# A two-layer decoder: the mix product with its weight stationary and in a new order, the sign weight made during the experts, the decay clamp on GpSimd

## The chip, the cores and the metric

The kernel runs on one core of a Trainium2 chip. The metric is the device time of one execution in microseconds (us). The engines that matter here are TensorE (PE; PEld is its weight load), VectorE (DVE), ScalarE (ACT) and GpSimd (POOL); SP only issues transfers.

## The reference, cut to what matters

The input x has 8 batches of 100 tokens and 256 features, the context 361 tokens for each batch. Six blocks follow one another, each on a layernorm of the stream x, each added to it: a self attention with contextual positions, a cross attention, a mixture of 8 experts, a gated recurrence, a cross attention with 16 heads, and a product with a ternary weight. The change touches blocks 4 and 6:

```python
aiv = x @ W_aiv                       # 256 -> 3 * 1024
a_proj, i_proj, v = jnp.split(aiv, 3, axis=-1)
a = jax.nn.sigmoid(a_proj + decay_bias)
i = jax.nn.sigmoid(i_proj)
input_signal = jnp.sqrt(jnp.maximum(1.0 - a * a, 1e-08)) * (i * v)
h = _chunked_scan(a, input_signal)    # along the 100 tokens, in chunks of 64
return h @ W_mix + b_mix              # 1024 -> 256
...
w_ternary = jnp.clip(jnp.round(w / scale), -1.0, 1.0)   # scale = max(mean |w|, 1e-5)
return jnp.einsum('bsi,oi->bso', x, w_ternary * scale)
```

## The kernel before

All engines have one instruction stream each, written by hand, and meet by semaphores. The program goes through the blocks in order.

**Experts and gather.** The experts' results go to memory (`slots_out`) and GpSimd fetches them back, one indirect DMA for each batch (L748). VectorE adds each to X (L1818), takes statistics and, for the first four batches, normalises as soon as GpSimd has made `rstd` by a power (`rsqrt(3, 0)`, L655, between the seventh and the eighth fetch). TensorE transposes the result into XT. Before that `side("gather")` makes the last value projections of block 5 and one column sum `f`, and `keep_warm` issues products that nobody reads.

**Recurrence.** The 1024 channels are 8 tiles j of 128 partitions; along the free axis lie 8 batches of 101 columns (one reset column each). TensorE makes for each j three gate products `aiv(n, g)` (L1388): the decay w=0, the input gate w=1, the value w=2, in two halves g of 400 tokens; the order is the list `AIV`. They use four pairs of PSUM banks, and item n waits until item n-4 was read. ScalarE turns w=0 and w=1 into DEC and UU by sigmoid (L967, L969), squares the clamped decay (L976) and takes the root (L980). VectorE does for each j: `decay(j)` = clamp of DEC to 1e-10..1 (L1838), one column for each batch into BT (L1845), a scan (L1848); `inputs(j-1)` = L1828 and the scan of the state L1831, after which `state` counts j; `gated(j)` = product with the value in PSUM (L1860, it gives `iv_done`) and L1862. After `gated(1)` it also makes the ternary weight WN (L1879 to L1884). GpSimd adds the mix bias to two batches of X (L768) after each of the first four states. It also clears the two BT buffers before the stage (L761 to L763).

**Mix product.** `mix(p, j)` (L1421) adds tile j to the result of the two batches of p, once `state` has reached j+1. UU is the stationary operand (100 tokens of one batch) and the 256 columns of W_mix move, so that the result lies with tokens on partitions and `x_add(p)` (L1892) adds it to X. TensorE does p=0 for all j, p=1 for all j, p=2 for all j, four half steps of p=3 (`mix_last`), and then starts block 5; twelve half steps of p=3 are filled into block 5's plan at ticks 0 to 22. After `x_add(p)` follow statistics, `rstd` on GpSimd (L774), normalisation (L1908), `x_tr(p)` (L1441), ScalarE's copy (L1008), the query product `q_mm(p)` (L1451), and `q_out(p)`, which gives the first of three bf16 parts of the queries. VectorE (p=0) or GpSimd (p=1 to 3) makes the other two parts; all are stored to memory and loaded back in another layout (L574, L440) before the first score product `maxima(0, 0)` (L1495) may start.

**Block 5** runs by the tables `PLAN` and `ONCE` in ticks, sixteen for a batch. For the first batch its first step is the row maximum on VectorE (L1934).

## Time and profile before

| | us |
|---|---|
| runs, median | 443.76 |
| runs, lowest and highest | 437.52, 448.41 |
| the profiled execution, its device time | 437.58 |
| its span, first to last instruction | 435.8 |
| gate products, start to end | 219.0 to 286.6 |
| mix products, start until block 5 starts | 286.6 to 316.6 |

The profile page gives a share of the span to each engine: PE 93%, DVE 61%, ACT 40%, POOL 31%. A window row gives the busy time of each engine in a stretch and the granted clock of TensorE, 1.00 for 2.4 GHz and 0.50 for 1.2 GHz. A timeline row gives start, length, engine, line, operation, operands and their shapes; `[2.00 <-DVE RC L1831]` behind it says that the engine was idle 2.00 us until that instruction ended. Three runs lie 11 us apart.

### The profile page before, as it was taken

To read this page: it belongs to the slowest core of one execution; us is meant where nothing else is said; L and a number is where in the kernel's file an instruction comes from. 1 tells how busy PE (TensorE), PEld (TensorE's weight loads), DVE (VectorE), ACT (ScalarE), POOL (GpSimd) and SP (SyncE) were. 2 spreads that over 40 slices of the span, in tenths; PEclk is the share of its full clock that TensorE was granted. 3 is DMA by queue.
4 is the path that set the end of the run, shared out by engine and by line. 5 is a ranking of instruction groups with operands and counts; after the bars stand their busy time and mean duration, and the time that the engine had idled before them with its cause. 6 is when DMAs were issued, how large, how long until landed. Compare 5 with 4: busy or idle time off the path is not lost.

```text
span 435.8 us, 7507 instructions
## 1 busy us (share of the span) xinstructions
PE 405.3 (93%) x2967; PEld 265.5 (61%) x2967; DVE 267.7 (61%) x475; ACT 174.9 (40%) x362; POOL 137.1 (31%) x188
## 2 busy tenths in 40 slices
PE   6999998995999998899699999989998999999896
PEld 2556664563556866697455555557765766666564
DVE  4159658899324552012855999992498677777334
ACT  0440351110431237342338367521105666666651
POOL 3852007763530044812700112000035473300200
PEclk9899999999999998999979999998999999999999
DMA  7994001111860065345200000055645437320001
GB/s 219 393 271 149 4 0 51 55 50 51 252 184 2 2 268 196 101 126 157 57 2 0 0 1 2 0 108 112 186 124 137 123 89 169 95 53 4 3 20 58
DMA packets 32850, 42.19 MB, mean 97 GB/s; under 512 B 7712, under 2 KB 29132, under 8 KB 32418
## 3 DMA queue, kind: packets, MB, share of 16 engines
q1 hardware_dynamic: 29897, 34.18, 26.5%
q0 software_dynamic: 2304, 5.76, 5.2%
q10 hardware_dynamic: 614, 1.77, 2.0%
q8 instruction: 24, 0.39, 0.4%
q14 instruction: 11, 0.09, 0.1%
HBM read 33.00 MB, written 8.98 MB: 96 GB/s over the span
## 4 chain that ended last, share of the span: by engine, by line
PE 56%; DVE 22%; issue 7%; DMA 5%; ACT 5%; POOL 3%; SPq 1%; POOLq 0%; DVEq 0%; ACTq 0%
PE banks L1421 5%; PE banks L1541 4%; PE banks L1105 4%; PE banks L1167 4%; PE banks L1526 4%; PE banks L1495 3%; PE banks L1255 3%; DVE NM L1934 3%; PE banks L1192 3%; PE banks L1388 2%; PE banks L1290 2%; PE banks L1308 2%; DVE RA L493 2%; DVE RC L1862 2%; DVE RC L1828 2%
## 5 line engine op out<-in xcount | busy, mean ns | idle before, releaser
L1934 DVE TENSOR_REDUCE NM<-banks 100x2 f32<-100x722 f32 x64 | 56.4, 903 | 19.5 <-PE banks L1495 19.2
L1388 PE MATMUL banks<-XT,RBG 128*128 128x400 f32 x192 | 67.3, 513 | 0.2 <-ACT XT L833 0.2
L1388 PEld LDWEIGHTS banks<-XT,RBG 128*128 128x128 f32 x192 | 37.4, 196 | 29.6 <-issue 3.1
L1046 ACT ACTIVATE CT<-banks 128x400 f32<-128x400 f32 (+1 forms) x72 | 35.8, 504 | 24.4 <-PE banks L1526 23.0
L1421 PE MATMUL banks<-W,RC 128*100 128x256 f32 x128 | 32.3, 395 | 2.0 <-DVE RC L1831 2.0
L1693 DVE TENSOR_TENSOR RC<-RV 128x800 f32<-128x800 f32 x16 | 19.3, 1278 | 14.2 <-ACT RV L875 14.2
L1421 PEld LDWEIGHTS banks<-W,RC 128*100 128x100 f32 x128 | 22.0, 175 | 8.3 <-DVE RC L1831 2.4
L1255 PE MATMUL banks<-RC,SELT 128*128 128x400 f32 x64 | 24.0, 508 | 2.7 <-DVE RC L1747 2.0
L1541 PE MATMUL banks<-CT,RV 128*17 128x100 f32 (+1 forms) x576 | 24.0, 254 | 0.0
L1616 DVE BATCH_NORM_STATS2 st<-X 100x6 f32<-100x256 f32 x48 | 19.5, 423 | 6.9 <-DMA X<-in_x 5.8
L655 POOL TENSOR_TENSOR rstd<-ve,mhalf 100x4 f32<-100x4 f32 x8 | 8.5, 1057 | 47.8 <-DVE ve L1625 47.8
L1145 PE MATMUL banks<-W,CT 128*128 128x256 f32 (+1 forms) x96 | 21.3, 381 | 0.7 <-DVE RC L1814 0.5
L1814 DVE TENSOR_TENSOR RC<-banks,RC 100x256 f32<-100x256 f32 x8 | 3.4, 424 | 28.6 <-PE banks L1377 28.6
L1145 PEld LDWEIGHTS banks<-W,CT 128*128 128x128 f32 (+1 forms) x96 | 17.5, 184 | 4.7 <-DVE RC L1814 0.9
L1255 PEld LDWEIGHTS banks<-RC,SELT 128*128 128x128 f32 x64 | 11.6, 189 | 12.8 <-DVE RC L1747 5.2
L768 POOL TENSOR_TENSOR X<-X,RB 100x512 f32<-100x512 f32 x4 | 5.1, 1272 | 45.5 <-DVE RC L1831 45.5
L1152 PE MATMUL banks<-onesb 128*128 128x512 bf16 x57 | 16.7, 435 | 2.4 <-POOL onesf L643 2.4
L1134 PE MATMUL banks<-CT,W 128*128 128x361 f32 x48 | 17.7, 521 | 1.1 <-issue 1.1
L1747 DVE TENSOR_TENSOR RC<-banks,RV 128x800 f32<-128x800 f32 x16 | 15.6, 984 | 4.2 <-PE banks L1255 4.2
L1526 PE MATMUL banks<-RC,RA 100*128 100x100 bf16 (+1 forms) x192 | 16.6, 210 | 1.3 <-DMA RC<-NT 1.3
L833 ACT ACTIVATE XT<-banks 128x800 f32<-128x800 f32 x8 | 6.6, 841 | 27.9 <-PE banks L1094 27.9
L774 POOL TENSOR_TENSOR rstd<-ve,mhalf 100x2 f32<-100x2 f32 x4 | 2.8, 702 | 46.9 <-DVE ve L1902 46.9
(259 smaller groups left out, 852.0 us busy)
## 6 DMA issues: line engine op xcount, KB each, us to landing
RA<-in_L_ffn_W SPq DMA_DIRECT2D x2, 2048.0 KB, 11.6
RBG<-in_L_attn_W_aiv SPq DMA_DIRECT2D x1, 3072.0 KB, 12.4
CT<-in_ctx_t SPq DMA_DIRECT2D x2, 1444.0 KB, 11.3
k_parts<-RA SPq DMA_DIRECT2D x12, 180.5 KB, 3.4
RA<-k_parts SPq DMA_DIRECT2D x12, 180.5 KB, 3.5
RBG<-k_parts POOLq DMA_DIRECT2D x12, 180.5 KB, 4.2
RA<-k_parts POOLq DMA_DIRECT2D x12, 180.5 KB, 3.9
RBG<-in_ctx SPq DMA_DIRECT2D x2, 1024.0 KB, 17.6
```

What stands on the lines that cost most here:

```text
L1046: sc.activation(P4[slot][0:n, g * HG * T:(g + 1) * HG * T], PS[4 + w % 2][0:n, 0:HG * T], ACT.Exp).then_inc(st_exp, 1)
L1105: ins = mm(bank[0:T, 0:D], lhs(k), rhs(k), start=(k == 0), stop=(k == KT - 1))
L1134: ins = mm((lo, hi)[m][:, 0:S], W4[:, 0, k, m * P:(m + 1) * P], CT[:, k, b * S:(b + 1) * S], start=(k == 0), stop=(k == KT - 1))
L1145: ins = mm(o, CT[:, k, b * S + s0:b * S + s0 + n], W4[:, 1, k, :], start=(k == 0), stop=(k == KT - 1))
L1255: ins = mm(PS[2 * (u % 2) + g][:, 0:GC], SELT[:, u], AL[:, GB * g:GB * g + GB].rearrange("p s t -> p (s t)"), start=True, stop=True)
L1388: ins = mm(PS[2 * aiv_pair(j, w) + g][:, 0:GC], WA[:, k, c:c + P], XT[:, k, GC * g:GC * g + GC], start=(k == 0), stop=(k == KT - 1))
L1421: ins = mm(PS[MIX_BANK[p]][0:T, b % 2 * D:b % 2 * D + D], UU[:, j, b, 1:TP], WMIX[:, j, :], start=(j == 0 and b % 2 == 0), stop=(j == RT - ...
L1526: ins = mm(PS[4 + w % 2][0:n, c * T:c * T + T], KS[b % KSLOTS][0:KROWS, h, s0:s0 + n], queries(KROWS, h, b), start=True, stop=True)
L1541: ins = mm(PS[6][32 * c:32 * c + VW, g * T:g * T + T], V4[0:n, NJ * b + j, h, :], P4[(NJ * b + j) % PSLOTS][0:n, h * T:h * T + T], start=( ...
L1616: v.bn_stats(st6[:, b], X[:, b]).then_inc(stats_done, 1)
L1693: v.tensor_tensor(PB[u % 5], k0[:, k].rearrange("p (s t) -> p s t", s=B), q0[:, k, s * T:s * T + T].unsqueeze(1).broadcast_to([P, B, T]), ...
L1934: v.tensor_reduce(NM[:, b % 2, 2 * i:2 * i + 2], PP[w % 2][0:T, :, 0:S], AX.X, ALU.max, negate=True).then_inc(mx_out, 1)
```

## The change

Three edits, with what they carry along.

1. **Mix product.** W_mix becomes the stationary operand (two halves of 128 output features), the 200 tokens of two batches move. The result has features on partitions. ScalarE copies it to XT (`mix_evac`), TensorE transposes it back into the same bank (`mix_tr`, four transposes), and `x_add` follows as before. TensorE's order is new: p=0 up to j=6, p=1 up to j=5, then (0,7), (1,6), (1,7), then `mix_tr(0)`, p=2, and twelve half steps of p=3, with the transposes and query products set between them. Four half steps of p=3 stay in the plan (ticks 0 to 3), `mix_evac(3)` and `mix_tr(3)` come at ticks 23 and 26. On VectorE `x_add(1)`, `ln_stats(1)` and `ln_norm(1)` now come ahead of the split of query 0.
2. **Sign weight.** WN is made while VectorE waits for the first expert. For that the column sum `f` moves from the last to the second place in the list `SIDE`. `keep_warm` ahead of the transposes of block 4 issues 14 products, not 5.
3. **Clamp.** For j of 2 and more, clamp and BT column are made by GpSimd, which also waits for `iv_done` of j-1. The four bias adds now follow the clamps of j=2 to 5. The clearing of BT moves from GpSimd to ScalarE, ahead of its first copy of XT; `rsqrt(3, 0)` comes after the eighth fetch.

```diff
-            keep_warm(PS[2], 5)
+            keep_warm(PS[2], 14)
...
             def mix(p, j, both=(0, 1)):
                 pe.wait_ge(state, j + 1)
-                for b in (2 * p + c for c in both):
-                    ins = mm(PS[MIX_BANK[p]][0:T, b % 2 * D:b % 2 * D + D], UU[:, j, b, 1:TP], WMIX[:, j, :],
-                             start=(j == 0 and b % 2 == 0), stop=(j == RT - 1), skip_group_check=True)
-                    if j == RT - 1:
-                        ins.then_inc(y_mm, 1)
+                for m in both:
+                    ins = mm(PS[MIX_BANK[p]][:, QC * m:QC * m + QC], WMIX[:, j, m * P:(m + 1) * P],
+                             UU[:, j, 2 * p:2 * p + 2, 1:TP], start=(j == 0 and m == 0), stop=(j == RT - 1),
+                             skip_group_check=True)
+                if j == RT - 1 and both[-1] == 1:
+                    ins.then_inc(mix_mm, 1)
                 return ins
+
+            def mix_tr(p):
+                pe.wait_ge(mix_out, p + 1)
+                for b in (2 * p, 2 * p + 1):
+                    for m in range(KT):
+                        c0 = b % 2 * D + m * P
+                        ins = nc.tensor.transpose(PS[MIX_BANK[p]][0:T, c0:c0 + P], XT[:, m, b * T:b * T + T], identf[:])
+                    ins.then_inc(y_mm, 1)
...
-            for j in range(RT):
+            for j in range(RT - 1):
                 mix(0, j)
-            for j in range(RT):
+            for j in range(RT - 2):
                 mix(1, j)
-                if j == 3:
-                    x_tr(0)
-                if j == 4:
-                    q_mm(0)
+            mix(0, RT - 1)
+            for j in (RT - 2, RT - 1):
+                mix(1, j)
+            mix_tr(0)
             pe.wait_ge(iv_done, RT - 1)
             for j in range(RT):
                 mix(2, j)
-                if j == 3:
-                    x_tr(1)
-                if j == 4:
-                    q_mm(1)
+                if j == 1:
+                    mix_tr(1)
+                elif j == 4:
+                    x_tr(0)
+                elif j == 5:
+                    q_mm(0)
...
-            for i in range(4):
+            for i in range(12):
                 ins = mix_last(i)
-            ins.then_inc(uu_used, 1)
+                if i == 3:
+                    ins.then_inc(mix_mm, 1)
+                    mix_tr(2)
+                elif i == 5:
+                    x_tr(1)
+                elif i == 7:
+                    q_mm(1)
...
+            def mix_evac(p):
+                act.wait_ge(mix_mm, p + 1 + p // 3)
+                src = PS[MIX_BANK[p]][:, 0:KT * QC].rearrange("p (k n) -> p k n", k=KT)
+                sc.activation(XT[:, :, QC * p:QC * p + QC], src, ACT.Copy).then_inc(mix_out, 1)
...
-                if b == B - 2:
-                    rsqrt(3, 0)
+            rsqrt(3, 0)
...
-            for p in range(B // 2):
+            def mix_bias(p):
                 pool.wait_ge(xn_ready, 4 * B)
-                pool.wait_ge(state, p + 1)
                 gp.tensor_tensor(X[:, 2 * p:2 * p + 2], X[:, 2 * p:2 * p + 2],
...
+            for j in range(2, RT):
+                pool.wait_ge(clamped, j)
+                pool.wait_ge(sig, SIG_AT[j, 0])
+                pool.wait_ge(iv_done, j - 1)
+                a_j, bt = DEC[:, j], BT[j % 2]
+                link(gp.tensor_scalar(a_j[:, :, 1:TP], a_j[:, :, 1:TP], FLOOR, 1.0, ALU.max, ALU.min))
+                gp.tensor_scalar(bt[:, :, 1 + CHUNK:2 + CHUNK], a_j[:, :, 1 + CHUNK:2 + CHUNK], 1.0 / FLOOR, None,
+                                 ALU.mult).then_inc(clamped, 1)
+                if j < 2 + B // 2:
+                    mix_bias(j - 2)
```

The order on VectorE in the recurrence, from `gated` of one tile to the scan of the decay two tiles on (RC holds UU, RA holds DEC, CT holds BT and the square roots; "x100" shapes are the clamp). Before:

```order
L1860 TENSOR_TENSOR RC<-RC,banks 128x8x100 [waits aiv_mm,sig]
L1862 SCALAR_TENSOR_TENSOR RC<-CT,RC 128x808 [waits iv_done]
L1838 TENSOR_SCALAR RA<-RA 128x8x100 [waits sig,dve_link]
L1845 TENSOR_SCALAR CT<-RA 128x8 [waits clamped]
L1848 SCALAR_TENSOR_TENSOR CT<-RA,CT 128x808 [waits dve_link]
L1828 SCALAR_TENSOR_TENSOR RC<-CT,RC 128x808 [waits roots,dve_link]
```

and after the change:

```order
L1907 TENSOR_TENSOR RC<-RC,banks 128x8x100 [waits aiv_mm,sig]
L1909 SCALAR_TENSOR_TENSOR RC<-CT,RC 128x808 [waits iv_done]
L1899 SCALAR_TENSOR_TENSOR CT<-RA,CT 128x808 [waits clamped,dve_link]
L1870 SCALAR_TENSOR_TENSOR RC<-CT,RC 128x808 [waits roots,dve_link]
L1873 SCALAR_TENSOR_TENSOR RC<-RA,RC 128x808 [waits u_done]
```

The clamp and the BT column are gone from VectorE, and its scan waits for `clamped`. On GpSimd, from the last fetch to the second tile, before:

```order
L748 DMA XN<-slots_out,small 100x256 x6
L655 TENSOR_TENSOR rstd<-ve,mhalf 100x4 [waits var_ready]
L748 DMA XN<-slots_out,small 100x256
L758 MEMSET RA 128x64 [waits k_st3,k_st2,side_mm]
L759 MEMSET RC 128x64
L761 MEMSET CT 128x808
L761 MEMSET CT 128x808 [waits pool_link]
L762 MEMSET CT 128x8 [waits pool_link]
L763 MEMSET CT 128x8
L655 TENSOR_TENSOR rstd<-ve,mhalf 100x4 [waits var_ready]
L768 TENSOR_TENSOR X<-X,RB 100x512 [waits state,xn_ready] x4
```

and after:

```order
L656 TENSOR_TENSOR rstd<-ve,mhalf 100x4 [waits var_ready]
L758 MEMSET RA 128x64 [waits k_st3,k_st2,side_mm]
L759 MEMSET RC 128x64
L656 TENSOR_TENSOR rstd<-ve,mhalf 100x4 [waits var_ready]
L772 TENSOR_SCALAR RA<-RA 128x8x100 [waits iv_done,sig,clamped]
L773 TENSOR_SCALAR CT<-RA 128x8 [waits pool_link]
L763 TENSOR_TENSOR X<-X,RB 100x512 [waits xn_ready]
L772 TENSOR_SCALAR RA<-RA 128x8x100 [waits iv_done,sig,clamped]
L773 TENSOR_SCALAR CT<-RA 128x8 [waits pool_link]
```

The power (`rstd`) moved behind the eighth fetch, the clearing of CT is gone, and a clamp (RA), a BT column (CT) and a bias add (X) now stand in turn, the clamp waiting for VectorE's `iv_done`.

On TensorE, what stands around the first transposes (banks2 is the bank pair of p=0 and p=1, banks3 that of p=2 and p=3, W0 holds W_mix, RC holds UU, W4 the query weights). Before, step (1,3), the transposes x_tr(0), step (1,4) and the query product q_mm(0):

```order
L1421 MATMUL banks2<-W0,RC 100x256 [waits state]
L1421 MATMUL banks2<-W0,RC 100x256
L1441 MATMUL banks0<-identf,XN 128x100 [waits xn_ready,sig]
L1441 MATMUL banks0<-identf,XN 128x100
L1441 MATMUL banks0<-identf,XN 128x100 [waits xn_ready]
L1441 MATMUL banks0<-identf,XN 128x100
L1421 MATMUL banks2<-W0,RC 100x256 [waits state]
L1421 MATMUL banks2<-W0,RC 100x256
L1451 MATMUL banks0<-XT,W4 128x200 [waits unit_xt]
L1451 MATMUL banks0<-XT,W4 128x200 x3
```

and after the change, step (1,7), mix_tr(0), the steps (2,0) and (2,1), and mix_tr(1):

```order
L1439 MATMUL banks2<-RC,W0 128x200 [waits state]
L1439 MATMUL banks2<-RC,W0 128x200
L1451 MATMUL banks2<-identf,XT 100x128 [waits mix_out]
L1451 MATMUL banks2<-identf,XT 100x128 x3
L1439 MATMUL banks3<-RC,W0 128x200 [waits state,iv_done]
L1439 MATMUL banks3<-RC,W0 128x200
L1439 MATMUL banks3<-RC,W0 128x200 [waits state]
L1439 MATMUL banks3<-RC,W0 128x200
L1451 MATMUL banks2<-identf,XT 100x128 [waits mix_out]
L1451 MATMUL banks2<-identf,XT 100x128 x3
```

`x_add(0)`, which came right behind step (0,7), now waits for mix_tr(0), with the steps (1,6) and (1,7) between them. The step (0,7), the first that needs the eighth state, stood eighth in the stream and now stands fourteenth; x_tr(0) moved from behind (1,3) to behind (2,4).

## Rows read from the trace of the kernel before

**Rows 1.** Busy time by stretch: window, length, five engines, granted clock, DMA share, GB/s

```profile
212.00:214.00 2.00, 0.00 (x0) 0.00 (x0) 1.78 (x7) 1.17 (x2) 1.04 (x1) 1.00 0.19 64
...
217.00:219.00 2.00, 1.45 (x5) 0.55 (x5) 1.93 (x7) 0.84 (x1) 0.28 (x3) 0.50 0.00 0
219.00:224.00 5.00, 5.00 (x8) 2.61 (x9) 2.93 (x11) 0.59 (x1) 1.04 (x1) 0.53 0.00 0
...
295.40:298.80 3.40, 3.40 (x10) 2.31 (x9) 1.80 (x7) 0.00 (x0) 0.53 (x1) 0.50 1.02 220
```

**Rows 2.** Timeline, last two state scans on VectorE, then TensorE

```profile
288.12 1.84 DVE L1831 TENSOR_TENSOR_SCAN RC<-RA,RC 128x808 f32<-128x808 f32 x1
...
292.94 1.84 DVE L1831 TENSOR_TENSOR_SCAN RC<-RA,RC 128x808 f32<-128x808 f32 x1
...
294.83 6.25 PE L1421 MATMUL banks<-W,RC 128*100 128x256 f32 x20 [2.00 <-DVE RC L1831]
```

**Rows 3.** Timeline of one tile of the scan: start, length, engine, line, shape [idle<-releaser]

```profile
253.91 0.96 DVE L1860 TENSOR_TENSOR RC<-RC,banks 128x800 f32<-128x800 f32 x1
254.14 1.27 POOL L768 TENSOR_TENSOR X<-X,RB 100x512 f32<-100x512 f32 x1 [8.68 <-DVE RC L1831]
...
254.91 1.36 DVE L1862 SCALAR_TENSOR_TENSOR RC<-CT,RC 128x808 f32<-128x808 f32 x1
...
256.30 0.58 DVE L1838 TENSOR_SCALAR RA<-RA 128x800 f32<-128x800 f32 x1
...
257.12 1.84 DVE L1848 TENSOR_TENSOR_SCAN CT<-RA,CT 128x808 f32<-128x808 f32 x1
...
260.03 1.84 DVE L1831 TENSOR_TENSOR_SCAN RC<-RA,RC 128x808 f32<-128x808 f32 x1
...
278.53 1.00 DVE L1862 SCALAR_TENSOR_TENSOR RC<-RA,RC 128x808 f32<-128x808 f32 x1
```

**Rows 4.** Timeline, VectorE, first and last of the six sign-weight instructions

```profile
246.34 0.15 DVE L1879 TENSOR_SCALAR fs<-fs 128x1 f32<-128x1 f32 x1
...
247.82 0.69 DVE L1884 TENSOR_TENSOR WN<-WN,WF 128x512 f32<-128x512 f32 x1
```

**Rows 5.** Timeline, TensorE, mix product, its transposes and the query product

```profile
286.62 6.21 PE L1421 MATMUL banks<-W,RC 128*100 128x256 f32 x28
...
300.91 0.51 PE L1441 MATMUL banks<-identf,XN 100*128 100x100 f32 x4
...
302.13 1.52 PE L1451 MATMUL banks<-XT,W 128*128 128x200 f32 x8
...
316.80 0.47 PE L1495 MATMUL banks<-RBG,RA 97*100 97x361 bf16 x2
```

**Rows 6.** Timeline around the last gather and the first gate products

```profile
213.89 3.38 DVE L1630 TENSOR_SCALAR XN<-X,mv,rstd 100x256 f32<-100x256 f32 x4
...
214.08 1.18 POOL L748 DMA_INDIRECT XN<-slots_out,small  x1 [0.23 <-issue]
...
219.00 5.28 PE L1388 MATMUL banks<-XT,RBG 128*128 128x400 f32 x8 [0.22 <-ACT XT L833]
...
220.62 1.38 DVE L1630 TENSOR_SCALAR XN<-X,mv,rstd 100x256 f32<-100x256 f32 x4 [1.17 <-POOL rstd L655]
```

**Rows 7.** Timeline of VectorE, then of GpSimd, where the two meet

```profile
65.52 1.85 DVE L1733 TENSOR_TENSOR RC<-RC,RA 128x800 f32<-128x800 f32 x1
...
66.58 1.43 POOL L694 CAST RA<-RA 128x722 bf16<-128x722 f32 x1
...
75.16 0.79 POOL L694 CAST RA<-RA 128x722 bf16<-128x722 f32 x1
```

**Rows 8.** Groups of instructions, GpSimd: count, busy us, mean ns

```profile
L709 POOL TENSOR_SCALAR mkx<-mki 8x361 bf16<-8x361 int32 x1 | 1.5, 1487 | 5.5 <-DMA mk<-in_mask_keep 5.5
```

**Rows 9.** Timeline of the SP queue, then the query loads of L440

```profile
307.93 1.88 SPq L440 DMA_DIRECT2D RA<-q_parts  x3
...
DMA to landing us min/median/max: 2.4/2.8/7.8
```

More of the change, by code:

```diff
@@ L330, in build @@
         q4_first = sem("q4_first")
-        uu_used = sem("uu_used")
+        mix_mm = sem("mix_mm")
+        mix_out = sem("mix_out")
         aiv_half = sem("aiv_half")
@@ L363, in __call__ @@
                 self.eng.wait_ge(self.sem, self.n)
-        SIDE = ([("qk", 0)] + [("k", b) for b in range(B)] + [("v", b) for b in range(B)] + [("f", 0)])
-        SIDE_AT = {"cope": 1, "soft": 3, "spread": 5, "ln1": 6, "ln2": 7, "router": 8, "route": 13, "gather": 18}
-        SIDE_LOW = [1, 3, 4, 8, 10, 12, 14, 16]
-        SPREAD_AT = {4: (3, 0), 5: (3, 1), 9: (4, 0), 10: (4, 1)}
+        SIDE = ([("qk", 0), ("f", 0)] + [("k", b) for b in range(B)] + [("v", b) for b in range(B)])
+        SIDE_AT = {"cope": 1, "soft": 4, "spread": 6, "ln1": 7, "ln2": 8, "router": 9, "route": 14, "gather": 18}
+        SIDE_LOW = [2, 4, 5, 9, 11, 13, 15, 17]
+        SPREAD_AT = {4: (4, 0), 5: (4, 1), 9: (5, 0), 10: (5, 1)}
         def side_bank(i):
@@ L405, in build @@
         PLAN_END = TICKS * (B - 1) + 60
-        ONCE = ([("mix_last", 2 * i if i < 14 else 2 * i - 11, 4 + i) for i in range(2 * RT - 4)]
-                + [("ln_norm", 15, 2), ("x_tr", 18, 2), ("x_out", 18, 2), ("q_mm", 20, 2), ("q_out", 20, 2),
+        ONCE = ([("mix_last", i, 12 + i) for i in range(4)]
+                + [("ln_norm", 15, 2), ("x_tr", 18, 2),
+                   ("x_out", 18, 2), ("q_mm", 20, 2), ("q_out", 20, 2), ("mix_evac", 23, 3), ("mix_tr", 26, 3),
                    ("x_add", 27, 3), ("zero_bank", 28, 0), ("ln_stats", 31, 3), ("ln_norm", 36, 3),
@@ L416, in build @@
         ORDER = ("q_mm", "x_tr", "x_out", "q_out", "x_add", "zero_bank", "ln_stats", "ln_norm", "parts", "sums_tr",
-                 "normalise", "out_tr", "out_mm", "maxima", "scores", "weighted", "os_evac", "add", "mix_last",
+                 "normalise", "out_tr", "out_mm", "maxima", "mix_evac", "mix_tr", "scores", "weighted", "os_evac", "add", "mix_last",
                  "last")
@@ L758, in _ @@
             gp.memset(DEC[:, :, :, 0:1], 0.0)
[L759 to L763 removed]
+            gp.memset(UU[:, :, :, 0:1], 0.0).then_inc(consts, 1)
             rsqrt(3, 1)
[L765 removed]
+            def mix_bias(p):
                 pool.wait_ge(xn_ready, 4 * B)
[L767 removed]
                 gp.tensor_tensor(X[:, 2 * p:2 * p + 2], X[:, 2 * p:2 * p + 2],
@@ L953, in _ @@
             sc.activation(BQ16[:, 0:1], BQ16[:, 0:1], ACT.Sigmoid)
+            for t in BT:
+                link(sc.activation(t, onesf[:, 0:1].unsqueeze(2).broadcast_to([P, B, TP]), ACT.Copy, scale=0.0))
+                sc.activation(t[:, :, 0:1], onesf[:, 0:1].unsqueeze(2).broadcast_to([P, B, 1]), ACT.Copy,
+                              scale=1.0 / FLOOR)
             xt_out(xn_tr, 3 * G, xt_ready, [0])
-            act.wait_ge(consts, 6)
+            act.wait_ge(consts, 7)
             def gate(j, w, groups=range(G)):
@@ L1027, in q_out @@
                 ins.then_inc(q4_out, 1)
+            def mix_evac(p):
+                act.wait_ge(mix_mm, p + 1 + p // 3)
+                src = PS[MIX_BANK[p]][:, 0:KT * QC].rearrange("p (k n) -> p k n", k=KT)
+                sc.activation(XT[:, :, QC * p:QC * p + QC], src, ACT.Copy).then_inc(mix_out, 1)
+            mix_evac(0)
+            mix_evac(1)
             x_out(0)
             q_out(0)
+            mix_evac(2)
             act.wait_ge(qs_one[0], 16)
@@ L1034, in _ @@
             q_out(1)
[L1035 removed]
+            act.wait_ge(mix_mm, NQ)
             load_queries(act, 1, 0)
@@ L1075, in last_xt @@
                 sc.activation(XT[:, :, b0 * T:b1 * T], src, ACT.Copy).then_inc(unit_xt, 1)
-            run_block4(scores=exps, parts=parts_out, os_evac=os_evac, out_tr=ot_evac, x_out=x_out, q_out=q_out,
+            run_block4(scores=exps, parts=parts_out, os_evac=os_evac, out_tr=ot_evac, x_out=x_out, q_out=q_out, mix_evac=mix_evac,
                        last_xt=last_xt)
@@ L1600, in _ @@
             run_block4(maxima=maxima, parts=parts_tr, scores=scores, weighted=weighted,
-                       sums_tr=sums_tr, out_tr=out_tr, out_mm=out_mm, mix_last=mix_last, x_tr=x_tr, q_mm=q_mm,
+                       sums_tr=sums_tr, out_tr=out_tr, out_mm=out_mm, mix_last=mix_last, mix_tr=mix_tr, x_tr=x_tr, q_mm=q_mm,
                        last_tr=last_tr, last_mm=last_mm, fill=lambda: keep_warm(PS[4], 2))
@@ L1851, in decay @@
             def decay(j):
-                dve.wait_ge(sig, SIG_AT[j, 0])
-                reset_scan(j, 1 if j < 2 else None)
+                if j < 2:
+                    dve.wait_ge(sig, SIG_AT[j, 0])
+                    reset_scan(j, 1)
+                else:
+                    dve.wait_ge(clamped, j + 1)
+                    link(v.tensor_tensor_scan(flat(CD[j % 2]), flat(DEC[:, j]), flat(BT[j % 2]), 0.0, ALU.mult,
+                                              ALU.max))
             def gated(j):
@@ L1913, in _ @@
             ln_norm(0)
+            x_add(1)
+            ln_stats(1)
+            ln_norm(1)
             dve.wait_ge(q4_out, 1)
@@ L1918, in _ @@
             v.tensor_tensor(QP[0][:, 2], QW[0], QP[0][:, 1], ALU.subtract).then_inc(q4_split, 1)
-            x_add(1)
-            ln_stats(1)
-            ln_norm(1)
             x_add(2)
```

32 lines of the change are left out of this document (12 added, 20 removed).

## The prediction

> **What bounds the kernel now.** I began with the chain of waits from the end. Between 286 and 317 us it leaves TensorE once: it goes back from the mix product to VectorE's last state scan. The timeline shows what that costs: TensorE has stood for 2.0 us when it starts at 294.83 [rows 2], and by the table of windows it then runs at clock 0.50 from 295.4 to 298.8 [rows 1]. VectorE is late because its tiles lie back to back: product 0.96, L1862 1.36, clamp and BT column 0.85, scan 1.84, 1.07 until the state scan, and that 1.84, together 7.9 us [rows 3]. The gate products don't wait for it, only the tail does. The second place is the start of the gate products: TensorE has nothing from 212 to 214, is at 0.50 by 217, and its first eight gate instructions take 5.28 us, 0.66 each, where the mean clock of the stretch is 0.53 [rows 1, 6]. The third is the mix stretch itself, where TensorE is the bound: it runs without a gap from 294.83 until the first score product at 316.80 [rows 2, 5].
>
> The sum is made against the profiled execution's 437.58 us. That is the fast end of the three runs; their median lies 6.2 us above it, so I carry the difference over as a ratio.
>
> **Gather and first gate products.** The eighth fetch (1.18 us) now comes ahead of the power, not behind it; the power waited for VectorE for about half of that, so I put the normalisation 0.6 later, at 214.5. The normalisation of four batches took 3.38 us while that fetch and the clearing of BT ran on GpSimd; the same four instructions without company take 1.38 [rows 6]. With 0.2 for two small clears beside it, it ends at about 216.1, not 217.3; with transposes and copy as before the products start at 217.45, not 219.00: -1.55. ScalarE's four fills of BT (two of 808 columns, for which VectorE's 1.00 [rows 3] is the nearest price, and two small ones, 2.4 in all) lie between its work before 214 and the copy of XT at 218 [rows 1]; without that cover they would cost 2.4. The nine extra warm products last to 213.5, in the hole of [rows 1] (212 to 214, no busy PE), so they cost nothing, and leave 4 us of sparse work ahead of the products, not 7. If the clock stays full, eight instructions need 0.33 us each, not 0.66: another -2.6, cut to -2.3 by the second normalisation, which now ends at 222.0 [rows 6] and then about 1.1 earlier. I take half of it, since the sparse stretch is shortened and not closed: **-2.8**, bounds -1.5 and -3.8. The sign weight leaves a busy VectorE for a stage in which it waits for the experts; its column sum is one product of one column, beside VectorE's softmax.
>
> **VectorE's tiles.** Removed: from the end of L1862 (256.27) to the scan (257.12) 0.85 a tile for six tiles, and the sign weight once, 246.34 to 248.51, less overlap 2.1 us [rows 3, 4]. Added: a wait for GpSimd. It gets `iv_done` when VectorE does, and VectorE starts L1862 0.04 us after L1860 [rows 3]. Where the two engines met in this trace, the one that came second stood still: L1862 takes 1.36 beside L768 and 1.00 without [rows 3]; a multiplication of 800 columns takes 1.85, and the GpSimd cast that starts while it runs takes 1.43 and ends 0.64 behind it, where the same cast takes 0.79 alone [rows 7]. So the clamp begins when L1862 ends, and VectorE waits for all of it. The clamp's price is not in the trace. Nearest is the cast of 722 columns, 0.79, one input and one output: 0.87 for 800. Far above lies the two-operation scalar instruction on integers, 1.49 for 361 columns [rows 8], which is 3.3 for 800. I take 1.0, by the cast, since data type, input count and shape are closer; both ends stay for the range. With 0.3 for the BT column and its wait and less 0.15 that the blocked start hides, the scan follows 1.2 us behind L1862: +0.35 for each of tiles 3 to 7, 1.8 in all, and +0.6 at tile 2, before which VectorE was idle. The four bias adds (1.27 [rows 3]) now queue right behind the clamps, beside scans with two inputs in SBUF. Each then blocks a scan or the L1828 behind it for 1.1, where it cost 0.36: +3.0. Bounds: 0 and -1.4 in place of +3.0 if scans don't collide with it. Sum: 1.8 + 0.6 + 3.0 - 2.1 = **+3.3** on the state of the last tile, measured from the gate products; bounds -1.0 and (clamp at 3.3 us, six times) +17. Queued behind the waiting clamp are the bias adds, for which only `x_add` waits.
>
> That GpSimd blocks or is blocked is what the Trainium skill says, "SBUF — State Buffer", section "Who interferes with whom": an operation of VectorE with two SBUF inputs and one of GpSimd that reads SBUF exclude each other, and the second waits for the whole of the first. The trace agrees (1.36 against 1.00). The page "GPSIMD Engine Reference", section "Engine selection", has GpSimd with one input at about line rate; an estimate by it, 800 columns at L1860's 0.96, would leave the sum as it is.
>
> **TensorE from the last gate product.** A step (p, j) was four instructions, 28 in 6.2 us or 0.87 a step; now it is four of 200 columns, as in the query product, where eight take 1.52 less about 0.17 by which the last overlaps the next: 0.675 [rows 5]. From 286.6 TensorE has six steps, 4.0 us, before it needs the state of tile 6; that came at 290.0 [rows 2], now 3.3 later, so it idles about 2.6 and then does seven steps in 4.7 and is at (0,7) just when the last state is (298.1). (0,7) began at 294.83: **+3.3**. The idle 2.0 was followed by 3.4 us at half clock [rows 1, 2]; I expect the same once: **+1.7**.
>
> From there to the first score product it was 316.8 - 294.8 = 22.0, of which 1.7 by the clock. Now: 17 steps 11.5, three `mix_tr` at 0.45 (x_tr is 0.51, less the same overlap 0.35, for 100 columns, these have 128), two x_tr 0.7, two query products 2.7: 16.2. But the queries arrive by memory: `x_tr(0)` and q_mm(0) come 7.3 after (0,7), as before (302.13), the last parts are loaded from 307.93, the third issue at 309.2, 14.4 us after (0,7), and land 2.8 later [rows 9], at 17.2, since nothing on that path got shorter. ScalarE's `mix_evac` (about 0.5 each) is covered by the two steps ahead of `mix_tr`. So 17.2, and 0.2 for the weight load ahead of the product, replace 22.0: **-4.6**. The eight half steps taken out of block 5's first ticks stood beside VectorE's row maxima; only the last of them, behind the maxima, holds the path: **-0.5**.
>
> Sum: -2.8 + 3.3 + 1.7 - 4.6 - 0.5 = -2.9, 434.7 us on the profiled execution, a ratio of 0.993, 440.8 on the median.
>
> **Rivals.** *GpSimd keeps clear.* If the bias adds fall beside L1860 (a PSUM input, 0.96 beside L768, not slowed [rows 3]) or scans don't collide, VectorE is 1.0 ahead, TensorE never waits, (0,7) starts 0.6 later only through its new place, and the clock holds: -2.8 + 0.6 - 4.6 - 0.5 = -7.3, 436.4. For it speaks that L1860 was not slowed, against it that each add is now released next to a scan. *The clamp is slow*, by the integer row: six tiles by 2.3 us is +13.8, 454.8 on the median. It decides from a clamp of 1.5 us (1.0 + 2.9 / 6). For it speaks that this row is the only one of its operation, against it the float rows, 1.1 ns a column for one input [rows 7] and 2.5 for two [rows 3]. *Nothing is gained*: the clock falls at 217 as before (-1.5 only), and block 5 takes back what comes early, since its transfers set the pace: 443.8 or 1 below.
>
> **How the numbers follow.** Forecast 0.43, GpSimd clear 0.25, nothing gained 0.15, slow clamp 0.17. The forecast is **440.8 us**. The range is 433.5 to 450: below, the clear case with a full clock at 219 (-8.3, 435.3) and some noise of the runs, which lie 11 us apart; above, a clamp of up to some 2 us; the worst of the slow clamp is left out. Faster by over 2%, about what a measurement of this kernel can tell from no change, means below 434.9: half of the clear case and noise, 0.18. Slower by over 2% is above 452.6: most of the slow clamp, 0.15. Within 2%: 0.67.
>
> **What would show it.** The first eight gate instructions start near 217.5 and take 2.7 or 5.3 us. L1899, the scan, starts 1.2 us after L1909; the clamp L772 shows 2.0 (1.0 blocked, 1.0 its own) and the bias L763 delays a scan or L1870. TensorE's gap before the mix product's seventh step is near 2.6 us, none before the fourteenth. The first score product starts 17 us after (0,7) and waits for a DMA. I am wrong if the clamp itself takes over 1.5 us, if TensorE waits inside the gate products, or if the gap before (0,6) is absent.

## The result and the profile after

| | before | after |
|---|---|---|
| median of 4 runs, us | 440.64 | 450.63 |
| lowest and highest, us | 434.27, 448.41 | 447.23, 451.26 |
| span of the profiled execution, us | 435.8 | 449.2 |
| TensorE's mean granted clock in it | 0.976 | 0.962 |

The ratio after to before is 1.032, 95% interval 1.021 to 1.043: the changed kernel is slower. The prediction, 440.8 us with a range up to 450.0, was wrong. What came true is the rival "the clamp is slow". Ratios here and below leave out executions more than 1.5% above the fastest of the same kernel, so they differ from the ratios of the medians (1.023 for this one), and the profiles of `undo_clamp` and `clamp_only` below are of executions that were left out.

The groups of instructions on GpSimd in the trace of after: line, engine, operation, shapes, count, busy us and mean ns of one, idle time ahead.

```profile
L772 POOL TENSOR_SCALAR RA<-RA 128x800 f32<-128x800 f32 x6 | 20.9, 3481 | 45.7 <-DVE RC L1907 28.6 <-ACT RA L977 17.1
```

The clamp takes 3.5 us on average, not the 1.0 that I took or the 2.0 that it was to show with the wait in it. One tile in the timeline of after shows what that does; it answers to [rows 3].

```profile
259.34 0.96 DVE L1907 TENSOR_TENSOR RC<-RC,banks 128x800 f32<-128x800 f32 x1
260.33 1.00 DVE L1909 SCALAR_TENSOR_TENSOR RC<-CT,RC 128x808 f32<-128x808 f32 x1
260.48 3.59 POOL L772 TENSOR_SCALAR RA<-RA 128x800 f32<-128x800 f32 x1 [5.67 <-DVE RC L1907]
264.16 0.25 POOL L773 TENSOR_SCALAR CT<-RA 128x8 f32<-128x8 f32 x1
264.36 1.27 POOL L763 TENSOR_TENSOR X<-X,RB 100x512 f32<-100x512 f32 x1
264.51 2.82 DVE L1899 TENSOR_TENSOR_SCAN CT<-RA,CT 128x808 f32<-128x808 f32 x1 [3.18 <-POOL CT L773]
267.37 1.00 DVE L1870 SCALAR_TENSOR_TENSOR RC<-CT,RC 128x808 f32<-128x808 f32 x1
268.40 1.84 DVE L1873 TENSOR_TENSOR_SCAN RC<-RA,RC 128x808 f32<-128x808 f32 x1
```

VectorE stands for 3.18 us behind L1909, not the 1.2 predicted, until the BT column is there. The bias add L763 then starts 0.15 us ahead of the scan, and the scan takes 2.82 where it took 1.84. From this clamp to the next (271.31) are 10.83 us, against 7.9 before.

TensorE in the same trace, from the first gate product to the first score product; it answers to [rows 2, 5, 6].

```profile
220.63 4.62 PE L1406 MATMUL banks<-XT,RBG 128*128 128x400 f32 x8 [0.64 <-ACT XT L839]
...
225.78 32.43 PE L1406 MATMUL banks<-XT,RBG 128*128 128x400 f32 x96
260.35 8.33 PE L1406 MATMUL banks<-XT,RBG 128*128 128x400 f32 x24 [2.15 <-DVE RC L1907]
271.17 10.02 PE L1406 MATMUL banks<-XT,RBG 128*128 128x400 f32 x24 [2.50 <-DVE RC L1907]
282.00 8.33 PE L1406 MATMUL banks<-XT,RBG 128*128 128x400 f32 x24 [0.80 <-DVE RC L1907]
291.84 5.64 PE L1406 MATMUL banks<-XT,RBG 128*128 128x400 f32 x16 [1.51 <-DVE RC L1907]
...
305.62 8.72 PE L1439 MATMUL banks<-RC,W 128*128 128x200 f32 x40 [3.87 <-DVE RC L1873]
...
329.70 0.48 PE L1530 MATMUL banks<-RBG,RA 97*100 97x361 bf16 x2 [0.22 <-ACT CT L1036]
```

A tile's 24 gate products need 8.33 us (the 10.02 are the same 24 with part of them at the lower clock). With VectorE at 10.83 a tile TensorE now waits inside them, four times, where before they ran without a gap, as this row of the kernel before shows:

```profile
224.80 61.98 PE L1388 MATMUL banks<-XT,RBG 128*128 128x400 f32 x184
```

### The profile page after: what moved, and what is told of

Same layout as the page of the kernel before. It is cut to its first block, busy times and chain, and to the rows that moved or that the text cites. A ratio compares the mean times of both kernels' runs of the same rounds, so it can differ in the third digit from the quotient of the medians.

```text
span 449.2 us, 7564 instructions
## 1 busy us (share of the span) xinstructions
PE 411.9 (92%) x2992; PEld 272.9 (61%) x2992; DVE 262.8 (59%) x463; ACT 178.4 (40%) x370; POOL 157.4 (35%) x196
## 4 chain that ended last, share of the span: by engine, by line
PE 58%; DVE 18%; POOL 7%; issue 6%; ACT 5%; DMA 4%; ACTq 0%; SPq 0%; POOLq 0%; DVEq 0%
PE banks L1576 5%; POOL RA L772 5%; PE banks L1561 4%; PE banks L1530 4%; PE banks L1185 4%; PE banks L1123 4%; PE banks L1152 3%; PE banks L1439 3%; PE banks L1273 3%; DVE NM L1972 3%; PE banks L1210 2%; PE banks L1308 2%; PE banks L1406 2%; PE banks L1326 2%; DVE RA L494 2%
## 5 line engine op out<-in xcount | busy, mean ns | idle before, releaser
L1406 PE MATMUL banks<-XT,RBG 128*128 128x400 f32 x192 | 69.4, 522 | 7.6 <-DVE RC L1907 7.0
L772 POOL TENSOR_SCALAR RA<-RA 128x800 f32<-128x800 f32 x6 | 20.9, 3481 | 45.7 <-DVE RC L1907 28.6
L1439 PE MATMUL banks<-RC,W 128*128 128x200 f32 x128 | 25.5, 351 | 3.9 <-DVE RC L1873 3.9
L1439 PEld LDWEIGHTS banks<-RC,W 128*128 128x128 f32 x128 | 23.2, 201 | 4.8 <-DVE RC L1873 4.4
L1152 PE MATMUL banks<-CT,W 128*128 128x361 f32 x48 | 20.7, 587 | 1.8 <-issue 1.1
L1170 PE MATMUL banks<-onesb 128*128 128x512 bf16 x66 | 18.7, 428 | 2.4 <-POOL onesf L644 2.4
L1163 PEld LDWEIGHTS banks<-W,CT 128*128 128x128 f32 (+1 forms) x96 | 17.6, 184 | 4.1 <-DVE RC L1856 0.9
L986 ACT ACTIVATE CT<-RA 128x808 f32<-128x808 f32 x8 | 6.9, 878 | 30.3 <-POOL CT L773 30.3
L1782 DVE TENSOR_TENSOR RC<-banks,RV 128x800 f32<-128x800 f32 x16 | 15.6, 983 | 4.7 <-PE banks L1273 4.5
L1185 PE MATMUL banks<-XT,W 128*128 128x400 f32 x48 | 17.4, 525 | 0.0
L694 POOL TENSOR_TENSOR RA<-RA 128x722 f32<-128x722 f32 x4 | 6.0, 1509 | 32.2 <-ACT RA L861 32.2
```

The lines of the kernel that those rows point to most:

```text
L772: link(gp.tensor_scalar(a_j[:, :, 1:TP], a_j[:, :, 1:TP], FLOOR, 1.0, ALU.max, ALU.min))
L1152: ins = mm((lo, hi)[m][:, 0:S], W4[:, 0, k, m * P:(m + 1) * P], CT[:, k, b * S:(b + 1) * S], start=(k == 0), stop=(k == KT - 1))
L1163: ins = mm(o, CT[:, k, b * S + s0:b * S + s0 + n], W4[:, 1, k, :], start=(k == 0), stop=(k == KT - 1))
L1185: ins = mm(PS[4 + i % 2][:, 0:GC], W0[:, w, k, m * P:(m + 1) * P], XT[:, k, GC * g:GC * g + GC], start=(k == 0), stop=(k == KT - 1))
L1406: ins = mm(PS[2 * aiv_pair(j, w) + g][:, 0:GC], WA[:, k, c:c + P], XT[:, k, GC * g:GC * g + GC], start=(k == 0), stop=(k == KT - 1))
L1439: ins = mm(PS[MIX_BANK[p]][:, QC * m:QC * m + QC], WMIX[:, j, m * P:(m + 1) * P], UU[:, j, 2 * p:2 * p + 2, 1:TP], start=(j == 0 and m == ...
```

## The experiments

Each was timed against the kernel before in five rounds, except `pairs`, which ran once, for its trace. "Tile period" is the distance from one tile's product to the next.

### The clamp back on VectorE: undo_clamp

The changed kernel, in which GpSimd's loop over the clamps is replaced by the bias adds as before, and:

```
             def decay(j):
-                if j < 2:
-                    dve.wait_ge(sig, SIG_AT[j, 0])
-                    reset_scan(j, 1)
-                else:
-                    dve.wait_ge(clamped, j + 1)
-                    link(v.tensor_tensor_scan(flat(CD[j % 2]), flat(DEC[:, j]), flat(BT[j % 2]), 0.0, ALU.mult,
-                                              ALU.max))
+                dve.wait_ge(sig, SIG_AT[j, 0])
+                reset_scan(j, 1 if j < 2 else None)
```

> The changed kernel with clamp, BT column and bias adds as they were before: the clamp on VectorE, each bias add on GpSimd released by a state scan. What stays is the mix product's new order, the early sign weight, the fills of BT on ScalarE and the 14 warm products. Theory (the clamp on GpSimd is the whole loss): tile period 7.9 us again (10.83 in the changed kernel), the product of the last state at most 1 us later after the first gate product than before (12 us later in the changed kernel), first score product 19 us behind the start of the step (0,7), and a time 4 to 7 us below the kernel before, ratio 0.985 to 0.990. Rival (the new order costs by itself, through idle TensorE and the half clock behind it): the score product no earlier than before, ratio 1.00 to 1.01.

Measured: median 432.5 us, ratio 0.987, interval 0.978 to 0.996. TensorE in its trace:

```profile
226.44 61.98 PE L1396 MATMUL banks<-XT,RBG 128*128 128x400 f32 x184
288.25 10.99 PE L1429 MATMUL banks<-RC,W 128*128 128x200 f32 x64
...
315.03 0.48 PE L1520 MATMUL banks<-RBG,RA 97*100 97x361 bf16 x2 [0.56 <-DMA RA<-q_parts]
```

The gate products run without a gap again. In the mix product 64 instructions, that is 16 steps, follow without a wait, so the states are always there first. The first score product comes 17.8 us behind (0,7), not 19, and waits 0.56 us for the queries' DMA. The later run

> The kernel undo_clamp once more, beside early_one and more_warm and against more runs of the kernel before, for a narrower interval. Theory (clamp on GpSimd is the whole loss, the rest a gain of 4 to 6 us): ratio 0.986 to 0.991. Rival (the rest gains nothing that can be measured): above 0.995.

gave 0.990, interval 0.982 to 0.997. Moving the clamp, with the bias adds queued behind it, turns a gain of about 1% into a loss of 3%.

### The clamp alone moved: clamp_only

The kernel before, with the changed kernel's `decay` and GpSimd's loop (the bias adds in it), and nothing else of the change.

> The kernel before with one part of the change alone: clamp and BT column on GpSimd, bias adds queued behind them. Theory (clamp is the whole loss): clamp 3.6 us when it starts beside L1862's 1.0 us, tile period 10.8, last state scan 12 to 14 us later after the first gate product, ratio 1.025 to 1.035. Rival (the new order has a share in the loss): ratio 1.01 to 1.02, less than the changed kernel shows.

Measured: ratio 1.033, interval 1.024 to 1.041, the same loss as the whole change. Its clamp takes 3.59 us, and TensorE waits inside the gate products and twice in the mix product (2.96 and 2.79 us). So the loss needs no share of the new order. Without the gain of the rest it might have been larger than the whole change's; the intervals, 2% wide, don't tell.

### One operation in place of two: one_op

```
-                link(gp.tensor_scalar(a_j[:, :, 1:TP], a_j[:, :, 1:TP], FLOOR, 1.0, ALU.max, ALU.min))
+                link(gp.tensor_scalar(a_j[:, :, 1:TP], a_j[:, :, 1:TP], FLOOR, None, ALU.max))
```

> The changed kernel with one operation in the clamp in place of two: the maximum stays, the minimum with 1 is left out (a sigmoid is never above 1, so the values are the same). Theory A (GpSimd pays by operation, about half for one): clamp 1.5 to 2.0 us in place of 3.6, tile period 9.0 to 9.3 us, time 9 us below the changed kernel, ratio to the kernel before 1.00 to 1.01. Theory B (the price is by element read and written, whatever is done to it): clamp 3.6, ratio to before 1.03 as with two.

Measured: ratio 1.013, interval 1.007 to 1.018. The clamp and TensorE's gap behind it in the trace:

```profile
265.54 2.92 POOL L772 TENSOR_SCALAR RA<-RA 128x800 f32<-128x800 f32 x1 [5.67 <-DVE RC L1907]
...
265.41 8.33 PE L1406 MATMUL banks<-XT,RBG 128*128 128x400 f32 x24 [1.82 <-DVE RC L1907]
```

Neither theory had the price. The second operation costs 0.67 us of 3.59, not half and not nothing. The tile period falls to 10.15 (255.26 to 265.41). Six clamps at 0.67 are 4.0 us. The ratio is 0.0195 lower than the changed kernel's, about 8.6 us, and the two intervals together leave 3 to 14. In the profiles the stretch from 225.78 (222.05 in one_op) to the first score product became 3.0 us shorter, which is the part that is seen to belong to the clamp; the rest of the 8.6 isn't shown to.

### The bias adds ahead of the clamps: bias_early

```
+            for p in range(B // 2):
+                mix_bias(p)
             for j in range(2, RT):
...
-                if j < 2 + B // 2:
-                    mix_bias(j - 2)
```

> The changed kernel with the four bias adds ahead of all clamps, where VectorE waits for the first gate values, in place of one behind each of the first four clamps. Theory A (each add blocks the scan of CD beside it: 2.82 us with, 1.84 without): scans 1.84 us in all tiles, tile period 9.85 from the start, last state scan 3.9 us earlier after the first gate product, time 4 us below the changed kernel, ratio to before about 1.02. Theory B (the scan is 2.8 us for another reason, such as the clamp that ended just before it): scans stay at 2.8, time as the changed kernel.

Measured: ratio 1.020, interval 1.013 to 1.028. The instructions of the scan's line: shortest, median and longest in ns.

```profile
L1900 DVE TENSOR_TENSOR_SCAN CT<-RA,CT x3: 1842/1843/1843, 244.4 to 283.8; 128x808 f32<-128x808 f32 x3
L1900 DVE TENSOR_TENSOR_SCAN RA<-RA,CT x3: 1841/1842/1843, 254.3 to 293.7; 128x808 f32<-128x808 f32 x3
```

All six scans take 1.84, where four took 2.82, and the tile period is 9.84 from the first tile on. Theory A holds: each bias add cost one scan 1.0 us.

### An earlier clamp: early_clamp and early_one

On top of bias_early, GpSimd waits for `iv_done` ahead of the BT column only:

```
                 pool.wait_ge(sig, SIG_AT[j, 0])
-                pool.wait_ge(iv_done, j - 1)
                 a_j, bt = DEC[:, j], BT[j % 2]
                 link(gp.tensor_scalar(a_j[:, :, 1:TP], a_j[:, :, 1:TP], FLOOR, 1.0, ALU.max, ALU.min))
+                pool.wait_ge(iv_done, j - 1)
```

> The kernel bias_early with GpSimd's wait for the product (iv_done) moved from ahead of the clamp to ahead of the BT column, so that the clamp may start as soon as ScalarE has written the gate. Theory A (GpSimd and VectorE's operations with two SBUF inputs exclude each other, so their times add up: 1.00 + 1.84 + 1.00 + 1.84 on VectorE, 2.93 + 0.25 on GpSimd, 8.86 us a tile, more than TensorE's 8.33): tile period 8.9 to 9.4 in place of 9.84, ratio to before 1.005 to 1.015, still slower. Theory B (only the clamp's late start costs): period 8.33 as TensorE sets it, ratio at most 0.99.

Measured: ratio 0.998, interval 0.994 to 1.001. The tile period alternates and comes to 8.63 (17.25 for two), less than theory A's sum. The trace shows where the sum fails:

```profile
257.72 1.00 DVE L1871 SCALAR_TENSOR_TENSOR RC<-CT,RC 128x808 f32<-128x808 f32 x1
257.77 3.69 POOL L774 TENSOR_SCALAR RA<-RA 128x800 f32<-128x800 f32 x1 [2.03 <-ACT RA L978]
258.55 0.90 ACT L980 ACTIVATE RC<-banks 128x400 f32<-128x400 f32 x2 [0.93 <-PE banks L1407]
258.76 2.37 DVE L1874 TENSOR_TENSOR_SCAN RC<-RA,RC 128x808 f32<-128x808 f32 x1
```

L1871 holds the clamp up by 0.76 (3.69 against 2.93 for the first clamp, which has no product beside it). The scan behind it then runs beside the clamp and loses only 0.53. Operations that shut each other out whole would need 1.00 + 1.84 + 2.93 = 5.8 us; these are done in 3.7. TensorE still waits 0.55 to 0.87 us every second tile inside the gate products and 1.12 in the mix product.

The same kernel with one operation in the clamp:

> The kernel early_clamp with one operation in the clamp in place of two (minimum left out, values the same). Theory A (the price of the clamp is what is left of the loss): VectorE's tile falls to TensorE's 8.33 us or under it, no gap inside the gate products, time as undo_clamp, ratio 0.987 to 0.991. Theory B (GpSimd's part in itself holds VectorE, whatever it costs): ratio 0.9975 as early_clamp.

Measured: ratio 0.992, interval 0.988 to 0.997, a gap of 0.17 us in two places of the gate products and one of 1.11 in the mix product. It lies between the theories' numbers, nearer to A. With an early release and a cheaper clamp no cost of the move is left that these intervals can tell, and it isn't seen to gain over the clamp on VectorE (0.987 and 0.990).

### The prices and collisions by themselves: pairs

Behind the last sum of undo_clamp, VectorE gives GpSimd and itself the same semaphore, once for each test, and each starts one operation.

> The kernel undo_clamp with 29 small tests appended behind its last sum, on buffers of 128 rows by 808 columns: six GpSimd operations alone (clamp with two operations, with one, with two on flat operands, product of two tiles, copy, fill), then each of clamp, product, copy and fill released by the same semaphore as a VectorE scan (two inputs in SBUF), a product of two tiles and a clamp on VectorE, then scan and product on VectorE released 0.4 us behind the GpSimd operation, then the three VectorE operations alone. Only durations are read, the time means nothing. Prices: clamp with two operations 2.93, with one 2.25 whether flat or not; product 2.0 (by the bias add, 1.27 for 512 columns); copy about 1.0 (by the cast, 0.79 for 722). Theory A (whichever engine is first, an operation of VectorE with two SBUF inputs and any of GpSimd exclude each other whole): the two ends lie apart so that the stretch from the first start to the last end is the sum, 4.8 us for scan and clamp, in both orders. Theory B (only VectorE shuts GpSimd out whole; a clamp, with one input, lets a scan that comes behind it run beside it, as a scan of early_clamp that took 2.37 us beside a clamp): scan behind clamp at most 2.4 us, scan behind GpSimd's product 2.8 to 3.8.

The timeline. L827 is the clamp with two operations, L828 with one, L829 with two on flat operands, L830 a product of two tiles, L831 a copy; on VectorE L2004 is the scan, L2006 a product, L2008 a clamp, L2017 a short clamp ahead of the late ones.

```profile
429.72 2.92 POOL L827 TENSOR_SCALAR RA<-RA 128x800 f32<-128x800 f32 x1 [7.46 <-DVE RC L2014]
432.85 2.21 POOL L828 TENSOR_SCALAR RA<-RA 128x800 f32<-128x800 f32 x1 [0.21 <-DVE RC L2014]
435.27 2.91 POOL L829 TENSOR_SCALAR RA<-RA 128x808 f32<-128x808 f32 x1 [0.21 <-DVE RC L2014]
438.38 1.88 POOL L830 TENSOR_TENSOR RA<-RA 128x808 f32<-128x808 f32 x1 [0.21 <-DVE RC L2014]
440.46 0.86 POOL L831 COPY RA<-RA 128x808 f32<-128x808 f32 x1 [0.19 <-DVE RC L2014]
...
442.43 1.84 DVE L2004 TENSOR_TENSOR_SCAN RC<-RC 128x808 f32<-128x808 f32 x1
442.48 4.45 POOL L827 TENSOR_SCALAR RA<-RA 128x800 f32<-128x800 f32 x1 [0.21 <-DVE RC L2014]
...
465.39 0.58 DVE L2008 TENSOR_SCALAR RC<-RC 128x808 f32<-128x808 f32 x1
465.45 3.26 POOL L827 TENSOR_SCALAR RA<-RA 128x800 f32<-128x800 f32 x1 [0.49 <-DVE RC L2014]
...
474.26 0.37 DVE L2017 TENSOR_SCALAR RC<-RC 128x400 f32<-128x400 f32 x1
474.31 3.04 POOL L827 TENSOR_SCALAR RA<-RA 128x800 f32<-128x800 f32 x1 [0.72 <-DVE RC L2014]
474.66 2.37 DVE L2004 TENSOR_TENSOR_SCAN RC<-RC 128x808 f32<-128x808 f32 x1
...
480.56 2.06 POOL L830 TENSOR_TENSOR RA<-RA 128x808 f32<-128x808 f32 x1 [0.61 <-DVE RC L2014]
480.92 3.40 DVE L2004 TENSOR_TENSOR_SCAN RC<-RC 128x808 f32<-128x808 f32 x1
...
484.58 1.05 POOL L831 COPY RA<-RA 128x808 f32<-128x808 f32 x1 [1.96 <-DVE RC L2014]
484.95 2.37 DVE L2004 TENSOR_TENSOR_SCAN RC<-RC 128x808 f32<-128x808 f32 x1
```

Theory B holds, with the copy cheaper than expected (0.86, not 1.0). Where VectorE is first, GpSimd stands for the rest of it: 1.53 us beside the scan (4.45 against 2.92), and 0.34 even beside VectorE's clamp of 0.58 us, which has one input. Where GpSimd is first, a scan that starts 0.35 behind waits 0.53 for a clamp and for a copy alike, and 1.56 for a product of two tiles (3.40 against 1.84). VectorE's product L2006 in the scan's place waits as long: 0.53, 0.53 and 1.56. So a clamp of 2.92 holds VectorE back until 0.9 us after its start, about as long as the whole copy takes. Some 0.1 to 0.2 us of that 0.9 are the clamp's own wait for L2017, which runs when it starts (3.04 against 2.92, copy 1.05 against 0.86).

The Trainium skill, "SBUF — State Buffer", section "Who interferes with whom", calls the shared ports an exclusive lock, and says of VectorE's 2-port modes that whoever issues first has them for the whole instruction. That is about so here with VectorE first and with GpSimd's product, and not with the clamp: it lets VectorE go after 0.9 of 2.9 us.

### The rest of the change in parts: mix_only and order_only

mix_only is undo_clamp with the sign weight back in VectorE's second tile. order_only is mix_only with GpSimd's clearing of BT, the power ahead of the eighth fetch and 5 warm products again.

> The kernel undo_clamp (clamp on VectorE) with the sign weight also back where it was, in VectorE's second tile. Theory A (in the new order TensorE has 13 steps of mix product before it needs the last state, so VectorE has slack and 2.1 us more on it show nowhere): as undo_clamp, ratio to before 0.985 to 0.99. Theory B (VectorE still sets the start of a step): 2.1 us above undo_clamp, ratio 0.992, with a gap of TensorE inside the first 14 steps of the mix product.

> As mix_only, and the part at the gather undone too: BT cleared on GpSimd again, the power between the fetches, 5 warm products. What stays of the change is the mix product's new order (with its transposes and copies). Theory A (the gather part gives 2.5 us, as the trace of the changed kernel has it): normalisation of four batches 3.4 us again, ratio to before 0.992 to 0.994. Theory B (the gather part gives nothing beyond the clock's chance): as mix_only, 0.987. If the order alone gives nothing: 1.00.

Measured: mix_only 0.988 (0.980 to 0.995), order_only 0.999 (0.995 to 1.002), medians 431.5 and 434.9 us on the same chip. In mix_only TensorE runs the first 16 steps of the mix product without a wait, as in undo_clamp, so no gain of the sign weight's new place is seen. The gather part is worth 3.4 us by the medians (the two intervals of their ratios lie just apart): in order_only the four normalisations take 3.39 us again, as in [rows 6]. What the order alone gives stays open. In the profiles it is 3.8 us from the last gate product to the first score product (26.35, before 30.18), by the ratio 0.5 us, between 2.1 gained and 1.1 lost, by the medians 1.6. The profiled execution of before had an idle of 2.0 us and a half clock behind it [rows 1, 2]; whether its other executions had them isn't to be seen.

### Clock: fill5 and more_warm

fill5 is undo_clamp with eight warm products between the first row maxima of block 5.

> The kernel undo_clamp with eight warm products (one of 512 columns each) spread between the first row maxima of block 5, where the kernel before had half steps of the mix product. Theory A (those half steps kept the clock up, and their removal is why block 5 gave nothing): clock 1.00 from the first score product to the third query product, that product 1.5 us and not 3.0, end 1 us earlier than in undo_clamp, ratio to before 0.983 to 0.986. Theory B (VectorE's row maxima and the transfers set the pace): clock up, time the same or a little longer, 0.987 to 0.989.

Measured: ratio 0.995 (0.991 to 0.998), median 434.4. First the windows of undo_clamp behind its first score product, then those of fill5; columns are PE, PEld, DVE, ACT and POOL busy, granted clock, DMA share and GB/s.

```profile
321.00:324.00 3.00, 2.28 (x10) 1.28 (x10) 2.98 (x5) 0.07 (x1) 0.99 (x4) 0.61 0.45 131
324.00:327.00 3.00, 3.00 (x10) 2.52 (x9) 0.91 (x1) 0.43 (x1) 0.00 (x0) 0.50 0.87 255
```

```profile
321.00:324.00 3.00, 2.72 (x16) 2.05 (x16) 1.69 (x3) 1.29 (x5) 0.00 (x0) 1.00 0.89 260
324.00:327.00 3.00, 3.00 (x19) 1.81 (x18) 2.88 (x5) 2.13 (x5) 2.43 (x4) 1.00 0.63 183
327.00:330.00 3.00, 1.57 (x18) 0.89 (x17) 2.15 (x5) 0.89 (x2) 2.41 (x2) 1.00 0.30 75
330.00:333.00 3.00, 2.94 (x35) 1.82 (x34) 2.97 (x8) 1.94 (x5) 1.19 (x4) 0.68 0.40 101
333.00:336.00 3.00, 3.00 (x37) 1.79 (x35) 1.69 (x4) 1.25 (x3) 0.30 (x2) 0.50 0.50 140
```

The half clock of undo_clamp at 321 to 327 is gone, and the third query product takes 1.62 us, not 3.03 (2.82 to 3.03 in the six profiles with the clamp on VectorE and without this filler). The kernel before had a clock of 1.00 from 316 to 340. But TensorE is then ahead of the transfers, stands for 1.32 us until the rows of the maxima have landed, and the half clock comes from 330 on. Nothing is gained, so theory A's 1 us is refuted. The time is above theory B's range too: by the medians fill5 is 2.9 us slower than mix_only beside it.

more_warm is undo_clamp with `keep_warm(PS[2], 18)` for 14 and `keep_warm(PS[4], 5)` for 2.

> The kernel undo_clamp with 18 warm products in place of 14 ahead of the transposes and 5 in place of 2 behind them, in gaps of 1.2 and 0.65 us. Theory A (the clock at the first gate products falls in about half of the executions because of these gaps: the first eight took 2.9 us in some profiles and 5.7 in others): they take 2.9 us, and the median is 1 to 1.5 us below undo_clamp, ratio 0.984 to 0.986. Theory B (the clock's fall has its cause elsewhere): ratio as undo_clamp.

Measured: ratio 0.985, interval 0.980 to 0.990, median 429.5 (undo_again beside it 432.7). TensorE at the first gate products:

```profile
209.39 4.05 PE L1160 MATMUL banks<-onesb 128*128 128x512 bf16 x18
213.77 1.36 PE L1102 MATMUL banks<-identf,XN 100*128 100x100 f32 x8 [0.33 <-DVE XN L1655]
214.96 1.24 PE L1160 MATMUL banks<-onesb 128*128 128x512 bf16 x5
216.20 2.92 PE L1396 MATMUL banks<-XT,RBG 128*128 128x400 f32 x8
```

The gaps of 1.0 to 1.2 and 0.65 us are down to 0.33 and nothing, and the eight products take 2.92. In the ten profiles here with 14 and 2 they took 2.92 or 2.93 in five and 4.47 to 5.67 in five, so one profile of more_warm can't tell its own spread. The two intervals overlap, so that it is better than undo_clamp isn't shown, and theory A stays open. It is faster than both kernels, the one before and the changed one.

## Why the prediction was wrong, step by step

| from the rows | predicted | in the profile after |
|---|---|---|
| up to the gather's first fetch | 0 | +3.5 |
| from there until the gate products run without a gap | -2.8 | -2.5 |
| from there to (0,7) | +3.3 and +1.7 | +16.3 |
| (0,7) to the first score product | -4.6 | -4.4 |
| block 5 | -0.5 | +0.5 |
| sum | -2.9 | +13.4 |

**The step that failed is the clamp's price.** "Nearest is the cast of 722 columns" and "I take 1.0, by the cast" put one row of GpSimd above another because data type and shape agreed. The integer row, the only one with that operation, gave 3.3; the clamp takes 2.92 alone. What it shared with that row, the kind of instruction, was what mattered: 0.86 for a copy and 2.21 for one operation with a constant, on the same tile. The Trainium skill, "GPSIMD Engine Reference", section "Engine selection", has GpSimd with one input at roughly line rate. The copy agrees (0.86 for 808 columns); the clamp, with one input too, takes over three times that.

**The rest of the term fits.** The clamp does wait for L1909: 0.66 blocked (3.59 against 2.93), of the 0.85 that were left of L1909. Four bias adds do cost a scan 1.0 us each, as bias_early shows. Put 2.93 in place of 1.0 for six clamps and the term is 3.3 + 11.6 = 14.9. Measured from the continuous gate products, the last state came 15.6 later with the products 1.0 later, 14.6. The point from which the rival decides, 1.5 us, wasn't tested; one_op, whose clamp of 2.25 still leaves the kernel slower, doesn't contradict it.

**TensorE's waits.** The gap before (0,6) is 3.87, not 2.6. Behind it the clock is 0.50 from 307 to 309 and 40 instructions take 8.72, 1.6 more than the 7.12 of early_clamp, so the +1.7 held. That TensorE waits inside the gate products was a sign named as against the forecast, and it came.

**The mix stretch held.** (0,7) starts 12 instructions of 0.17 ahead of the transposes at 314.18, at 312.1, and the first score product is 17.6 behind it; 17.4 were predicted. The path isn't quite the predicted one: in the profile after the product's last wait, 0.22 us, is for ScalarE's L1036 behind the second query product, not for the queries' DMA, so that sign didn't come and part of the match is luck. In undo_clamp it is 17.8 with 0.56 of it a wait for that DMA. **The gather part held**: normalisation 1.38 us, -2.5 in the profile, 3.4 by the medians of mix_only and order_only. The first gate products started 1.9 earlier against the first fetch and ran at half clock for part of their time (4.62), as the halved term has it. The sum itself was off: a normalisation that ends 1.2 earlier doesn't give 1.55, and with half of 2.3 on top the term is -2.3, nearer to the profile's -2.5 and further from the 3.4.

**Block 5 gave nothing.** From the first score product to the end the profiles have 119.0 before, 119.5 after, 118.4 to 119.5 in the kernels with the clamp on VectorE (123.1 in fill5). The half steps that were taken out had filled TensorE's gaps between the row maxima. Without them the clock is halved there (0.50 from 339 to 342 in the profile after), and with filler it is halved behind the next transfer (fill5). The -0.5 counted work that was taken away, and not what its absence does.

**The sign weight** was booked at -2.1. mix_only shows no cost in its old place while the clamp is on VectorE: in undo_clamp the last state is there at 294.4 and is needed at 297.2, so VectorE has 2.8 us to spare.

**The 3.5 us ahead of the gather** aren't the change's: early_clamp and more_warm, with the same instructions there, reach the first fetch at 201.94 and 201.74, the kernel before at 202.87, the changed one at 206.36. In the changed kernel's profiled execution TensorE had a clock of 0.75 and 0.66 in two stretches (110 to 120 and 160 to 170 us), where before had 0.94 and 0.83. Which of the two kernels meets that more often isn't told by a profile.
